# Transposes of weights, tokens and down tiles by DMA, and a rearranged front, in a gated state-space and ternary-FFN kernel

## What is computed

```python
x1 = einsum('ed,bld->bel', in_proj_w, ctx);  u = silu(conv4(x1) + conv_b)
dt, B, C = split(x_proj_w @ u, [8, 16, 16]);  delta = softplus(dt_proj_w @ dt + dt_proj_b)
state = state * exp(delta * A) + (delta * u) * B     # 256 time steps, 256 channels x 16 states
y = (sum_n state * C + D * u) * silu(norm(x))
x2 = x + tanh(g_xattn) * y
h = quant(norm(x2)) @ ternary(w_gate).T,  quant(norm(x2)) @ ternary(w_up).T
out = x2 + tanh(g_ffn) * (quant(fwht(silu(h0) * h1)) @ ternary(w_down).T)
```

## Time and profile before

| | us |
|---|---|
| median of 3 runs (lowest, highest) | 221.41 (221.14, 222.14) |
| the profiled execution | 220.58 |
| its span, first to last instruction | 218.8 |
| DVE busy | 188.0 (86%) |
| PE busy | 188.9 (86%) |
| ACT busy | 168.9 (77%) |
| POOL busy | 108.0 (49%) |
| loads and stores | 6.33 MB, nearly all in the first 20 us |

### The profile page before, as it was taken

How to read it: one execution, slowest core, us unless ns; L and a number is a source line. 1 busy time by engine, 2 the same in 40 slices (tenths; PEclk the granted TensorE clock), 3 DMA queues, 4 the chain that set the end, 5 groups by cost and what they waited for, 6 DMA issues and landing times. The chain is left out here.

```text
span 218.8 us, 3665 instructions
## 1 busy us (share of the span) xinstructions
PE 188.9 (86%) x1221; PEld 152.7 (70%) x1228; DVE 188.0 (86%) x290; ACT 168.9 (77%) x298; POOL 108.0 (49%) x143
## 2 busy tenths in 40 slices
PE   2747889999899999899999999998998987686773
PEld 1534567887697998578989897797885776653751
DVE  1384938899999999998999999999989996889983
ACT  0278799999989969898967989993997811895373
POOL 1004700678708388029998991299920489510000
PEclk9965599999999999999999999999999999999998
DMA  5894000000000000000000000000000000000001
GB/s 135 264 343 182 0 1 4 0 0 0 3 0 0 3 1 1 0 3 0 1 3 0 0 3 24 1 27 0 0 0 3 25 0 27 0 0 0 27 24 48
DMA packets 8147, 6.33 MB, mean 29 GB/s; under 512 B 2202, under 2 KB 7874, under 8 KB 8130
## 3 DMA queue, kind: packets, MB, share of 16 engines
q1 hardware_dynamic: 6066, 6.01, 8.4%
q10 hardware_dynamic: 2064, 0.10, 0.6%
HBM read 5.05 MB, written 1.05 MB: 28 GB/s over the span
## 5 line engine op out<-in xcount | busy, mean ns | idle before, releaser
L1036 ACT ACTIVATE decay<-delta,zero_c,aneg 128x255 f32<-128x255 f32 x128 | 65.8, 588 | 1.6 <-DVE delta L1686 1.4
L1611 DVE TENSOR_TENSOR_SCAN state<-decay,BC 128x512 f32<-128x512 f32 x32 | 38.8, 1212 | 5.6 <-PE BC L397 3.8
L1611 DVE TENSOR_TENSOR_SCAN state<-decay,UP 128x512 f32<-128x512 f32 x32 | 38.4, 1201 | 1.1 <-issue 0.6
L1694 DVE TENSOR_TENSOR prod<-state,BC 128x1024 f32<-128x1024 f32 x32 | 38.4, 1200 | 0.7 <-PE BC L444 0.5
L1498 POOL TENSOR_TENSOR wnat<-wnat 128x512 f32<-128x512 f32 x18 | 22.9, 1275 | 26.2 <-DVE wnat L1738 25.4
L397 PE MATMUL BC<-diagB,duT 128*128 128x256 f32 x128 | 33.7, 386 | 0.7 <-DVE state L1611 0.5
L460 PE MATMUL PY<-id,prod 128*128 128x128 f32 x256 | 33.2, 273 | 1.1 <-DVE prod L1694 1.1
L397 PE MATMUL UP<-diagB,duT 128*128 128x256 f32 x128 | 33.3, 382 | 0.0
L460 PEld LDWEIGHTS PY<-id,prod 128*128 128x128 f32 x256 | 29.2, 141 | 3.9 <-DVE prod L1694 1.7
L397 PEld LDWEIGHTS BC<-diagB,duT 128*128 128x128 f32 x128 | 22.3, 190 | 5.2 <-issue 2.0
L397 PEld LDWEIGHTS UP<-diagB,duT 128*128 128x128 f32 x128 | 22.7, 190 | 3.6 <-issue 1.2
(11 more groups left out here) (250 smaller groups left out, 383.1 us busy)
## 6 DMA issues: line engine op xcount, KB each, us to landing
xs<-in_x_dram SPq DMA_DIRECT2D x1, 1024.0 KB, 8.8
wnat<-in_L_ffn_w_gate_dram SPq DMA_DIRECT2D x1, 1024.0 KB, 12.0
wnat<-in_L_ffn_w_up_dram SPq DMA_DIRECT2D x1, 1024.0 KB, 14.5
wnat<-in_L_ffn_w_down_dram SPq DMA_DIRECT2D x1, 1024.0 KB, 13.9
out_dram<-ot SPq DMA_DIRECT2D x8, 128.0 KB, 1.7
ctxs<-in_ctx_dram SPq DMA_DIRECT2D x1, 384.0 KB, 4.3
ctxs<-in_ctx_dram SPq DMA_DIRECT2D x1, 128.0 KB, 2.9
inw<-n_L_xattn_in_proj_w_dram SPq DMA_DIRECT2D x1, 128.0 KB, 2.6
```

Source lines behind the costliest of these rows:

```text
L1036: last = nc.scalar.activation(decay[:, m % RING, h, n, 1:L], delta[:, b % 2, h, 1:L], ACT.Exp, bias=zero_c[:], scale=aneg[:, h, NB * j + n ...
L1611: nc.vector.tensor_tensor_scan(state[:, g % STATES, h].rearrange("p n l -> p (n l)"), decay[:, g % RING, h].rearrange("p n l -> p (n l)"), ...
L1694: nc.vector.tensor_tensor(prod[:, g % RING].rearrange("p h n l -> p h (n l)"), state[:, g % STATES].rearrange("p h n l -> p h (n l)"), PC. ...
```

## The change

**Transposes.** Three functions on SP, `turn_weights(m)`, `turn_tokens(f)` and `turn_down(f, t)`, each issue one DMA with transpose from SBUF to SBUF. They take the place of `weight_T`, `tokens_T` for f = 0 to 2 and `q2_T` for f = 0 and 1 on PE, of `tokens_out_early` and `q2_out_early` for these on ACT, and of the six `weight_out` on DVE. A new `weight_floor(m)` on DVE does the bound at -1 in place before the turn. q2 of batch 2 and all of batch 3 stay on PE. The layouts of wT and qT change with it, and the stores of the output share SP's queue with the turns.

**Front.** dtb and dskip are loaded by SP (dtb behind x, dskip last of all loads). ACT's order puts `silu_u(0)` ahead of `tanh_gates`, and `dt_rows(0)` ahead of `inw_out` and `ctx_out`; DVE picks rows first. PE gets products of a tile of ones with itself, `warm` (11 calls) and `warm_later` (5 calls), two products each, whose results nobody reads.

**Order.** The orders of PE, ACT, POOL and DVE are written out anew throughout.

```diff
+            def turn_weights(m):
+                sp.wait_ge(dve_wq, m + 1)
+                sp.dma_start(wT[:, m].rearrange("p (k c) -> p k c", c=P), wq[:, m], transpose=True).then_inc(turned_w, 16)
+            def turn_tokens(f):
+                sp.wait_ge(dve_q, f + 1)
+                if f >= 1:
+                    sp.wait_ge(pe_up, LC * f)
+                sp.dma_start(qT[:].rearrange("p t h c -> p (t h) c"), q[:].rearrange("p t e -> p (t e)"), transpose=True
+                             ).then_inc(turned_q, 16)
+            def turn_down(f, t):
+                sp.wait_ge(dve_q2, LC * f + t + 1)
+                if f >= 1:
+                    sp.wait_ge(pe_dn, LC * (f - 1) + t + 1)
+                sp.dma_start(q2T[:, t], q2[:, t], transpose=True).then_inc(turned_d[t], 16)
...
+            turn_weights(0)
+            turn_tokens(0)
+            turn_weights(1)
+            turn_weights(2)
+            turn_down(0, 0)
+            turn_tokens(1)
+            turn_down(0, 1)
+            turn_down(1, 0)
+            store(0, 0)
+            turn_tokens(2)
+            store(0, 1)
+            store(1, 0)
+            turn_down(1, 1)
...
+            def warm(i):
+                if i == 0:
+                    pe.wait_ge(consts, 1)
+                for n in range(2):
+                    nc.tensor.matmul(X[:, P * n:P * (n + 1)], onesf[:], onesf[:], start=True, stop=True)
+            def warm_later(i):
+                pe.wait_ge(act_setup, 2)
+                for n in range(2):
+                    nc.tensor.matmul(PB[:, P * n:P * (n + 1)], onesf[:], onesf[:], start=True, stop=True)
...
             def gate(f, t):
-                pe.wait_ge(act_qT, f + 1)
+                pe.wait_ge(turned_q, 16 * (f + 1))
                 if f == 0 and t == 0:
-                    pe.wait_ge(dve_wT, 6)
+                    pe.wait_ge(turned_w, 16 * 3)
+                    pe.wait_ge(act_spread, 2)
                     pe.wait_ge(act_duT, 2)
...
+            def weight_floor(m):
+                dve.wait_ge(dve_wr, m + 1)
+                nc.vector.tensor_scalar(wq[:, m], wq[:, m], -1.0, None, ALU.max).then_inc(dve_wq, 1)
```

More of the change, by code:

```diff
@@ L316, in _ @@
             sp.dma_start(xs[:].rearrange("p b c d -> p (b c) d"), tiles(x)).then_inc(ld_x, 16)
+            with nc.allow_non_contiguous_dma(reason="one value per partition"):
+                sp.dma_start(dtb[:], dt_proj_b.rearrange("(h p) -> p h", p=P)).then_inc(ld_dtb, 16)
             sp.dma_start(wnat[:, 0].rearrange("p (a h) -> p a h", a=NI),
@@ L896, in _ @@
             drive_rows(28, 1)
+            drive_rows(29, 0)
+            C_rows(27)
+            accumulate(25)
             accumulate(26)
-            C_rows(27)
-            q2_T(1, 0)
-            tokens_T(2)
             gate(2, 0)
-            drive_rows(29, 0)
             drive_rows(29, 1)
@@ L970, in setup_loads @@
                 act.dma_start(alog[:], A_log.rearrange("(h p) n -> p h n", p=P)).then_inc(ld_gate, 16)
-                with nc.allow_non_contiguous_dma(reason="one value per partition"):
-                    for dst, src in ((dtb, dt_proj_b), (dskip, D)):
-                        act.dma_start(dst[:], src.rearrange("(h p) -> p h", p=P)).then_inc(ld_conv, 16)
                 nc.scalar.preload_act_table_set("silu_and_others")
@@ L1240, in _ @@
             dtw_out()
+            silu_u(0)
             tanh_gates()
-            silu_u(0)
-            inw_out()
-            ctx_out()
             for_exp()
             dt_rows(0)
+            exp_A()
+            inw_out()
             high_pieces(0)
+            spread(0)
+            ctx_out()
+            softplus(0)
+            weight_abs(0)
             first_rstd()
-            spread(0)
-            exp_A()
-            softplus(0)
             copy_BT(0)
-            weight_abs(0)
             decays(0, 0)
@@ L1908, in _ @@
             times_C(4)
-            weight_means()
             scan(6, 0)
@@ L1913, in _ @@
             scan(7, 0)
+            weight_means()
             scan(7, 1)
+            times_C(6)
             weight_round(0)
-            weight_round(1)
-            weight_out(0)
-            times_C(6)
+            weight_floor(0)
             scan(8, 0)
@@ L1923, in _ @@
             scan(9, 1)
-            weight_out(1)
             times_C(8)
             scan(10, 0)
-            weight_round(2)
+            weight_round(1)
             residual(0)
-            weight_out(2)
+            scan(10, 1)
             stats2(0, dve_ln_link)
-            weight_out(3)
-            scan(10, 1)
+            weight_floor(1)
             times_C(9)
@@ L1936, in _ @@
             times_C(10)
+            scan(12, 0)
             token_scale(0, dve_ln_link)
-            weight_out(4)
-            scan(12, 0)
             scan(12, 1)
-            weight_out(5)
+            weight_round(2)
             round_tokens(0)
+            weight_floor(2)
             times_C(11)
@@ L2015, in _ @@
             scan(29, 1)
+            round_down(1, 1)
             times_C(28)
             gate_times_up(2, 0)
-            result(1, 0)
             scan(30, 0)
```

456 lines of the change are left out of this document (213 added, 243 removed).

## The result

The changed kernel takes 232.5 us (median of 4 runs, 231.2 to 233.1) against 221.3 us before (4 runs, 220.2 to 222.1): ratio 1.0506 [1.0455, 1.0556], 11.2 us slower. The forecast had the sign, 223.4 us, but the time lies 2 us above its range, 215.5 to 230.5.

A forecast was written before the change was run, and what follows sets the result against it. DVE was taken to bound the body, working 144.5 of 151.7 us. 220.58 - 3.1 - 1.7 - 2.0 + 5.7 + 2.1 + 1.0 = 222.6, plus 0.83 is 223.4 us; range 215.5 to 230.5.

The forecast's parts named there:

- Part 4: Later turns of tokens and down tiles in the body: only down(0,1) and down(1,0) cost, +2.1 us (0 to 3.8).
- Part 2: Less work on DVE, PE and ACT: -1.7 us of DVE work and -2.0 us of waits.
- Part 1: The front: loads moved to SP and new orders bring the first scan from 31.74 to 28.6 us, -3.1 us.
- rival 4: The front gains nothing because the clock stays at 1.2 GHz: 226.5 us, chance 0.07.
- Waits shortened: Work taken off PE and ACT shortens DVE's 7.2 us of waits in the body: -2.0 us (0 to -5).
- Part 3: gate(0,0) waits for the weights' turns, held back behind turn_tokens(0) on SP: stall +5.7 us (3.3 to 11.4).
- D: Time from the end of weight_floor(2) to the last weight turn's landing: 6.1 us; the stall is D-0.4.
- My two prices: DMA costs from the queue rows: 18.6 ns per 256-byte run on 16 engines, plus 1.3 us fixed.
- Part 5: PE's clock may fall to 1.2 GHz in the stall at gate(0,0): +1.0 us (0 to 2.0).
- Rival 1: Weights turned as fast as loaded (D 3.7, stall 3.3), clock holds, it ends faster: 218.4 us, chance 0.28.
- rival 3: No stall at gate(0,0): DVE reaches the point late or turns land at once; 214.6 us, chance 0.08.
- Rival 2: SP's issuing of the turns is the bound: stall 11.4, clock 2.0, 230.1 us, chance 0.15.

The follow-up runs named there:

- before_front_noprod: The kernel before with the whole new front but without the products of ones, no turn by DMA: 217.8 us, ratio 0.9849.
- ahead_kept: turns_ahead without the token turns of batches 1 and 2 and without the down-tile turns after down(0,0)'s: 218.4 us, ratio 0.9858.
- turns_ahead: The changed kernel with weight_round(2) and weight_floor(2) ahead of token_scale(0), and SP turning all three matrices before the tokens: 225.7 us, ratio 1.0202.
- pool_waits: The changed kernel with POOL held back before softplus_tail(2,1) until weight_floor(2) is done: 231.35 us, ratio 1.0431.
- w_early: The changed kernel with all three weight turns reading matrix 0 right after weight_floor(0), tokens turned last: 225.4 us, ratio 1.0191.
- front_wturn: The kernel before with the new front (no products) and only the three weight matrices turned by DMA: 217.2 us, ratio 0.9798.
- w1_first: The changed kernel with turn_weights(1) ahead of turn_tokens(0) on SP, nothing else: 231.1 us, ratio 1.0407.
- tokens_kept: The changed kernel without turn_tokens(1) and turn_tokens(2), gates of batches 1 and 2 using batch 0's turned tokens: 231.4 us, ratio 1.0409.

## Why the forecast was wrong, step by step

Two steps of the forecast failed. Part 4 took the later turns of tokens as hidden behind a quant_down and priced all later turns at 2.1 us; they cost 6.3. Part 2 counted 3.7 us for less work and shorter waits; next to none of it reached the end. A third cost, POOL beside DVE's roundings, was put at nothing without a reason and took 2.1 us in the changed kernel.

The forecast's terms beside what the ends of the kernels give. Each measured value is the difference of two ends: the first row's kernel against the kernel before, and each later row's against the kernel of the row above.

| term | forecast | measured (end) | from |
|---|---|---|---|
| front | -3.1 | -3.3 | before_front_noprod |
| less work, shorter waits | -3.7 | +0.9, with 1.6 us wait for the first tokens in it | ahead_kept |
| later turns | +2.1 | +6.3 | turns_ahead |
| weights' turns, clock in the stall | +6.7 | +4.5 | pool_waits |
| POOL beside DVE's roundings | 0 | +2.1 | the changed kernel |
| sum | +2.0 | +10.5 | |

The last two rows together, 6.6 us, are what the turns of the weights cost here; how they divide depends on the order in which the causes are taken away, as w_early shows. The 6.7 forecast also holds the tokens' turn, whose 1.6 us stand in the second row.

**Part 1 held.** dt_rows(0) was forecast at 14.8 and ran at 14.52, the decays at 23.6 and ran at 22.65, the first scan at 28.6 and came at 27.91. The clock was at full from 12 us on. The one thing overstated was the products: the prediction's rival 4 put the whole 3.1 us on the clock, and without them, at 1.2 GHz, the first scan came 0.24 us later. And the cover of diag_D was a fact of the new order only, as the kernel with the loads alone showed.

**Part 2 failed for the most part.** weight_floor costs 0.69 us beside an idle POOL (0.6 forecast), so DVE's work is shorter as said. That it counts for the end was the wrong step: front_wturn removes just this, with the 48 transposes of PE, and gains 0.2 us. DVE's busy share of 95% in the body had made me price its work at full value. The same row has PE at 145 us of 151.7, and front_wturn took 1.35 us of work from DVE and 1.0 from PE; both only stood idle for longer. What holds the steps in their place there is not shown. "Waits shortened", -2.0, had no row behind it, and no kernel shows it.

**Part 3 was right in mechanism and size, and blind to a second cost.** D was forecast at 6.1 us and was 6.7 (weight_floor(2) ended at 85.7, gate(0,0) began at 92.38). With this D the formula gives 6.3 us of stall. DVE waited 7.03 us for C_rows(12) and 0.51 for the drive behind it, 7.5 in all, and the gate and the accumulate at the low clock, 1.6 us longer on PE, are more than the difference. The list of issues gives the median from issue to landing:

```profile
q2T<-wq SPq DMA_TRANSPOSE x4, 3.1
wT<-wq SPq DMA_TRANSPOSE x3, 4.4
qT<-q SPq DMA_TRANSPOSE x3, 2.4
```

They carry 256, 512 and 128 KB. My two prices gave 2.5, 3.7 and 1.9, each 0.5 to 0.7 us short. From 128 to 512 KB the landing grows by 2.0 us, which is 5.1 us per MB or about 195 GB/s. The price by packets was near. The page's line of the queue in the changed kernel, beside the earlier trace rows, and a window of the stall (PE busy, clock, DMA share, GB/s):

```profile
q1 hardware_dynamic: 18706, 9.02, 15.1%
...
88.00:92.00 4.00, 0.00 (x0) 0.59 1.07 198
```

This queue has 12640 packets and 3.0 MB more than before. About 540 of the packets came over from q10, where dtb and dskip were, so the turned tiles go in pieces of some 250 bytes, and by the shares of the engines' time a piece took about 21 ns, where 18.6 was forecast. With a share of 1.07 the DMA engines were full at 198 GB/s, so the transfer itself held the last turns. The Trainium skill, Advanced Engine Details and Errata, section X-Bar Transpose (TRN2), has such DMAs as fast as plain ones, 350 to 400 GB/s; the trace doesn't agree, as a window of plain loads shows 389 GB/s and the turns, with the engines as busy, 198. The held-back turn was named as the reason for the stall, and w1_first shows it: 2.6 us for one matrix. What the forecast missed is that DVE's three instructions just ahead of the turns would run beside POOL's: +3.0 us on DVE, 2.1 at the end. Before, the weights' rounding took 1.2 us each time; what POOL would do beside it in the new order was not looked up.

**Part 4 failed in size and in one named step.** Of gate(1,0) and gate(2,0) it said "both also wait for a quant_down of ACT that ends about then"; that was wrong. In the changed kernel gate(1,0) waits 2.31 us and gate(2,0) 1.69, both put down to the DMA of qT. The quant_down of ACT had ended 2.4 and 2.1 us before these gates, at 135.9 and 174.2 us. Down(0,1) and down(1,0) were forecast at 1.1 and 1.0 us and waited 0.68 and 1.66. So the waits of the two down tiles were sized about right, and the two token tiles that I had taken as hidden wait for longer, 4.0 us against 2.3. tokens_kept shows why it is not simply their sum: what one turn's wait gives up, the next takes.

**Part 5** was about right: the clock stood at 0.50 from 89 to 95 us, and gate(0,0) and the accumulate behind it took 1.87 and 1.79 us instead of 1.04 each, 1.6 us on PE against 1.0 forecast. With the stall gone (turns_ahead) the clock stayed at 1.00.

**The rivals.** Rival 1 (turned as fast as loads) falls by the landing times, rival 3 by the stall, rival 4 by the first scan. Rival 2 came near in the time (230.1), but by luck: SP issued two weight turns in 4.40 us and a token turn in 1.19, and D was 6.7, not 11.8; what brought the time up were the later turns. The range was too narrow because its upper end was one large stall; it had no case in which the later turns cost three times their price while the gain of part 2 stays away.

## What to carry to other kernels

A transfer that stands between a producer and its consumer can cost up to its landing time (here 2.4 to 4.4 us for a turned tile) unless the producer can be moved that far ahead. The weights could be moved, and then cost nothing; tokens and down tiles, which are read as soon as they are made, were not, and cost 6 to 7 us. In one in-order DMA queue, issue by the time the input is ready: a turn that stood behind a later one made its reader wait 2.6 us longer. Work saved on a busy engine is not yet time saved: 1.35 us less on DVE turned into 1.35 us more of waiting. And before moving roundings on DVE, look at what POOL does in that stretch.

The best kernel of the study is the one before with the new front, with or without the weights' turns by DMA: 217.2 to 218.8 us, 1.5 to 2% faster than before.

## What was not expected of the hardware

- Roundings on DVE of 1.20, 0.43 and 0.69 us took 2.21, 1.49 and 1.57 us with POOL working beside them. The scans and products (1.2 us) did not change in the same stretch. In the kernel with the front alone a rounding of the tokens took 1.42 us in one run and 0.43 in the other, with POOL's diagonals recorded as starting 0.05 and 0.06 us behind it. That it is the same effect is argued, not shown.
- Three turns of 512 KB issued one after another at once (w_early) held SP's queue for 8.23 us, and their median from issue to landing was 5.7 us, not 4.4. The DMA engines were full meanwhile (61 to 65 us: share 1.14, 207 GB/s), so they wait for one another there.
- The granted clock fell to 0.50 while PE stood still for some 7 to 9 us at the turns. In the changed kernel it was back at 1.00 at 96 us, within 4 us of the restart, but in tokens_kept the second gate, 3.8 us after the restart, still ran slow. With waits of 3.35 us (w_early) and 1.6 us (turns_ahead) at the same place it never fell. In the front it was 0.50 in one kernel and 1.00 in another with nearly the same work.
